# Expert layer of a decoder: the expert's columns as the stationary operand, and each tile's expert weights loaded into a ring of four

## The reference

```python
logits = x @ router_w + router_b
route = jax.nn.softmax(logits, axis=1)
max_prob = jnp.max(route, axis=1, keepdims=True)
max_ind = jnp.argmax(route, axis=1)
for e in range(num_experts):                    # 8
    h = x @ w1[e]                               # 128 -> 1024
    a, g = jnp.split(h, 2, axis=1)              # 512 each: "gate" a, "up" g
    y = jax.nn.silu(a) * g @ w2[e]              # 512 -> 128
    out = jnp.where((max_ind == e)[:, None], y, out)
out = out * max_prob                            # and the layer adds its input x
```

## Time and profile before

| what | value |
|---|---|
| median of 3 runs | 1973.05 us |
| profiled execution / its span | 1976.97 / 1975.2 us |
| PE, DVE, ACT, POOL busy, whole span | 1752.9, 1389.3, 1320.4, 854.7 us |
| expert phase: first row load issued / last output scatter | 1685.32 / 1966.79 us into the span |
| DMA over the whole span | 74.60 MB, mean 38 GB/s |

### The profile page before, as it was taken

The page is one execution under the profiler, slowest core; times in us unless marked ns, Lnnn a source line. Parts: engine busy times, 40 slices in busy tenths (PEclk is TensorE's granted clock), DMA queues, the critical chain, the costliest instruction groups (busy, mean ns, idle before and its releaser), DMA issues. The chain is left out here.

```text
span 1975.2 us, 52932 instructions
## 1 busy us (share of the span) xinstructions
PE 1752.9 (89%) x13247; PEld 1494.5 (76%) x13248; DVE 1389.3 (70%) x4484; ACT 1320.4 (67%) x3660; POOL 854.7 (43%) x2194
## 2 busy tenths in 40 slices
PE   5777679999997999979999999699999994788887
PEld 3444468888886999967888888588888883677776
DVE  5777658878876888866887887588888885233332
ACT  4444368888884777757888887588888883333343
POOL 1222044554541222224555453467877776133232
PEclk9999779999998999988999999899999997899999
DMA  8980000000000000000000000001111110111110
GB/s 233 391 345 0 1 14 12 12 13 12 12 11 2 0 0 0 0 1 1 0 0 0 0 0 1 21 24 28 34 32 31 32 33 31 30 35 33 33 33 21
DMA packets 76443, 74.60 MB, mean 38 GB/s; under 512 B 33077, under 2 KB 61896, under 8 KB 76368
## 3 DMA queue, kind: packets, MB, share of 16 engines
q1 hardware_dynamic: 71760, 64.85, 10.2%
q0 software_dynamic: 4320, 8.53, 1.2%
q10 hardware_dynamic: 288, 0.34, 0.1%
HBM read 30.02 MB, written 44.12 MB: 38 GB/s over the span
## 5 line engine op out<-in xcount | busy, mean ns | idle before, releaser
L1039 PE MATMUL xa_ps_o<-xa_vb,xa_pt 128*128 128x96 f32 x2048 | 246.6, 274 | 0.0
L1039 PEld LDWEIGHTS xa_ps_o<-xa_vb,xa_pt 128*128 128x128 f32 x2048 | 239.4, 192 | 0.1
L884 ACT ACTIVATE xa_pt<-xa_ps_pt 128x512 f32<-128x512 f32 x256 | 139.1, 595 | 96.5 <-PE xa_ps_pt L958 96.5
L1206 PE MATMUL ffn_ps_h<-ffn_xdt,w1t 128*128 128x128 f32 x1536 | 184.4, 276 | 0.4 <-ACT ffn_xdt L1172 0.4
L1287 DVE TENSOR_TENSOR exp_hg<-exp_silu,exp_ps_u 128x256 f32<-128x256 f32 x142 | 59.8, 421 | 174.0 <-ACT exp_silu L1272 174.0
L696 DVE TENSOR_REDUCE xa_mx<-xa_ps_s 128x8 f32<-128x512 f32 x256 | 164.9, 686 | 22.5 <-PE xa_ps_s L974 19.0
L1206 PEld LDWEIGHTS ffn_ps_h<-ffn_xdt,w1t 128*128 128x128 f32 x1536 | 178.9, 194 | 0.7 <-ACT ffn_xdt L1172 0.7
L848 POOL TENSOR_TENSOR xa_km<-xa_kt,const_sb 128x256 f32<-128x256 f32 x256 | 152.6, 617 | 36.5 <-ACT xa_kt L897 28.7
L702 DVE TENSOR_TENSOR xa_pr<-xa_ps_s,xa_mx 128x512 f32<-128x512 f32 x256 | 163.6, 680 | 0.2
L974 PE MATMUL xa_ps_s<-xa_km,xa_qm 64*128 64x256 f32 x1024 | 149.0, 410 | 4.0 <-POOL xa_km L848 4.0
L878 ACT ACTIVATE xa_pr<-xa_pr 128x512 f32<-128x512 f32 x256 | 147.2, 622 | 3.7 <-DVE xa_pr L702 0.8
(11 more groups left out here) (273 smaller groups left out, 4708.4 us busy)
## 6 DMA issues: line engine op xcount, KB each, us to landing
x_sorted<-no_row SPq DMA_DIRECT2D x1, 34320.0 KB, 91.2
xa_cn<-in_ctx_dram SPq DMA_DIRECT2D x128, 64.0 KB, 1.8
exp_xg<-x_sorted SPq DMA_DIRECT2D x71, 66.0 KB, 1.8
w1e<-in_L_ffn_w_dram SPq DMA_DIRECT2D x1, 4096.0 KB, 14.4
xa_mi<-in_mask_BxSxS_ik_dram SPq DMA_DIRECT2D x128, 32.0 KB, 2.2
out_dram<-exp_y,exp_token POOLq DMA_INDIRECT x71, 2.3
x_sorted<-x_sb,place POOLq DMA_INDIRECT x64, 2.4
x_sb<-in_x_dram SPq DMA_DIRECT2D x1, 512.0 KB, 5.2
```

Source lines behind the costliest of these rows:

```text
L884: nc.scalar.activation(pt[:, 512 * hf:512 * hf + 512], ps_pt[hf][:, :], ACT.Copy).then_inc(s["pt_sb"], 1)
L1039: last = nc.tensor.matmul(ps_o[:, 2 * VW * g:2 * VW * g + av_w], pt[:, P * g:P * g + P], vb[(r + 1) % RING][:, 2 * VW * g:2 * VW * g + av_ ...
L1206: last = nc.tensor.matmul(ps_h[c][:, 0:P], k.w1t[:, j, c, :], xdt[:, :, j:j + S], start=j == 0, stop=j == 2)
```

## The change

In `experts` the roles of the operands in UP are swapped. A 128-column piece of the expert's w1 is now stationary and the transposed tile `xt` moves, so the result comes out with the inner channel on the partitions, as Y needs it for its stationary operand. The transposes of `hg` and the copy `ht` are gone. Gate and up each get a PSUM tile of their own (512 wide, four pieces of 128), silu and the product are one instruction each over 512 columns, and `xt`, `silu`, `hg`, `ps_g`, `ps_u` and `ps_y` are doubled. On DVE `xn` now stands ahead of `hg`, on ACT `xt` ahead of silu.

The experts' weights no longer stay in SBUF. For each tile SP reads the owner's number and loads that expert's w1 (128 rows of 4 KB) and w2 (128 x 4 rows of 512 bytes) into one of four slots, for tile t+3 in turn t, once Y of tile t-1 has read the slot. PE waits for both loads before UP. The two loads of all experts in the first phase are gone, and with them the two register reads on PE.

```diff
+WRING = 4
 def load_weights(nc, k, a, sp):
-    sp.dma_start(k.w1e[:, :].rearrange("p (e f) -> p e f", e=E), a["L1_ffn_w1"].rearrange("e d f -> d e f")
-                 ).then_inc(k.expert_weights, 16)
-    sp.dma_start(k.w2e[:, :].rearrange("p (e c n) -> p e c n", e=E, c=FC),
-                 a["L1_ffn_w2"].rearrange("e (c p) n -> p e c n", p=P)).then_inc(k.expert_weights, 16)
...
             def _(sp):
                 def body(t, r):
...
                         sp.dma_start(xg[(r + 4) % XRING][:, :], k.x_sorted[bass.ds(first, P), :]).then_inc(s[f"x_in{r % 2}"], 16)
+                    if live(t + 3):
+                        e = sp.value_load(k.owner[0:1, col(t + 3)], min_val=0, max_val=E - 1)
+                        q = (r + 3) % WRING
+                        wait(sp, s["y_done"], t)
+                        sp.dma_start(w1b[q][:, :], w1[bass.ds(e, 1), :, :].rearrange("one d f -> d (one f)")
+                                     ).then_inc(s[f"w_in{q}"], 16)
+                        sp.dma_start(w2b[q][:, :, :], w2[bass.ds(e, 1), :, :].rearrange("one (c p) n -> p (one c) n", p=P)
+                                     ).then_inc(s[f"w_in{q}"], 16)
...
             def _(pe):
...
+                    if live(t + 1):
+                        q = (r + 1) % 2
+                        w = w1b[(r + 1) % WRING]
+                        pe.wait_ge(s["t_sb"], t + 2)
+                        pe.wait_ge(s[f"w_in{(r + 1) % WRING}"], 8 * (t + 1 - (r + 1) % WRING) + 32)
+                        wait(pe, s["hg"], t)
+                        for c in range(FC):
+                            last = nc.tensor.matmul(ps_g[q][:, c * P:(c + 1) * P], w[:, c * P:(c + 1) * P], xt[q][:, :],
+                                                    start=True, stop=True)
+                        last.then_inc(s["gate_done"], 1)
+                        for c in range(FC):
+                            last = nc.tensor.matmul(ps_u[q][:, c * P:(c + 1) * P], w[:, F + c * P:F + (c + 1) * P], xt[q][:, :],
+                                                    start=True, stop=True)
+                        last.then_inc(s["up_done"], 1)
                     if live(t):
-                        pe.wait_ge(s["hg"], 2 * t + 2)
-                        wait(pe, s["ht_sb"], t)
+                        q = r % 2
+                        pe.wait_ge(s["hg"], t + 1)
+                        wait(pe, s["y_sb"], t - 1)
                         for c in range(FC):
-                            last = nc.tensor.transpose(ps_ht[:, c * P:(c + 1) * P], hg[:, c * P:(c + 1) * P],
-                                                       k.const[:, C_ID:C_ID + P])
-                        last.then_inc(s["ht_done"], 1)
...
+                            last = nc.tensor.matmul(ps_y[q][:, 0:D], hg[q][:, c * P:(c + 1) * P], w2b[r % WRING][:, c, :],
                                                     start=c == 0, stop=c == FC - 1)
                         last.then_inc(s["y_done"], 1)
```

More of the change, by code:

```diff
@@ L948, in _ @@
                 if route:
-                    pe.wait_ge(k.expert_weights, 64)
+                    pe.wait_ge(k.expert_weights, 32)
                 kv = P if cross else 0
@@ L1213, in _, with experts @@
                 pipeline(pe, nt, 5, body, unroll=4)
-def experts(nc, k, out):
+def experts(nc, k, out, w1, w2):
     nt = k.nt
@@ L1230, in ps @@
             return ctx.enter_context(nc.psum_tensor("exp_ps_" + name, [P, w], F32))
-        half = F // 2
         xg = [sb(f"xg{i}", [P, R]) for i in range(XRING)]
+        w1b = [sb(f"w1b{i}", [P, 2 * F]) for i in range(WRING)]
+        w2b = [sb(f"w2b{i}", [P, FC, D]) for i in range(WRING)]
         xn = sb("xn", [P, D])
[L1234 to L1237, removed]
+        xt = [sb(f"xt{i}", [P, P]) for i in range(2)]
+        sa = [sb(f"silu{i}", [P, F]) for i in range(2)]
+        hg = [sb(f"hg{i}", [P, F]) for i in range(2)]
         y = [sb(f"y{i}", [P, D]) for i in range(2)]
@@ L1240, in experts @@
         token = [sb(f"token{i}", [P, 1], I32) for i in range(2)]
+        ps_g = [ps(f"g{i}") for i in range(2)]
         ps_u = [ps(f"u{i}") for i in range(2)]
-        ps_t, ps_ht, ps_y = (ps(n) for n in ("t", "ht", "y"))
-        names = ["x_in0", "x_in1", "xn", "t_done", "t_sb", "up_done", "silu", "hg", "ht_done", "ht_sb", "y_done", "y_sb",
-                 "carried", "stored0", "stored1"]
+        ps_y = [ps(f"y{i}") for i in range(2)]
+        ps_t = ps("t")
+        names = ["x_in0", "x_in1", "xn", "t_done", "t_sb", "gate_done", "up_done", "silu", "hg", "y_done", "y_sb",
+                 "carried", "stored0", "stored1"] + [f"w_in{i}" for i in range(WRING)]
         s = {n: k.sem("exp_" + n) for n in names}
@@ L1263, in body @@
                 def body(t, r):
[L1264 to L1273, removed]
                     if live(t + 2):
                         act.wait_ge(s["t_done"], t + 3)
-                        wait(act, s["up_done"], 2 * t + 4)
-                        nc.scalar.activation(xt[:, :], ps_t[:, 0:P], ACT.Copy).then_inc(s["t_sb"], 1)
+                        wait(act, s["up_done"], t + 1)
+                        nc.scalar.activation(xt[r % 2][:, :], ps_t[:, 0:P], ACT.Copy).then_inc(s["t_sb"], 1)
+                    if live(t + 1):
+                        q = (r + 1) % 2
+                        act.wait_ge(s["gate_done"], t + 2)
+                        wait(act, s["hg"], t)
+                        nc.scalar.activation(sa[q][:, :], ps_g[q][:, :], ACT.Silu).then_inc(s["silu"], 1)
                 pipeline_ring(act, ne, 4, body, XRING)
@@ L1282, in body @@
                 def body(t, r):
[L1283 to L1288, removed]
                     if live(t + 3):
@@ L1295, in body @@
                                                 ALU.subtract, ALU.mult).then_inc(s["xn"], 1)
+                    if live(t + 1):
+                        q = (r + 1) % 2
+                        dve.wait_ge(s["silu"], t + 2)
+                        dve.wait_ge(s["up_done"], t + 2)
+                        wait(dve, s["y_done"], t)
+                        nc.vector.tensor_tensor(hg[q][:, :], sa[q][:, :], ps_u[q][:, :], ALU.mult).then_inc(s["hg"], 1)
                     if live(t):
@@ L1300, in body @@
                         dve.wait_ge(s["y_done"], t + 1)
-                        nc.vector.scalar_tensor_tensor(y[q][:, :], ps_y[:, 0:D], row[:, GATE:GATE + 1], row[:, 0:D],
+                        nc.vector.scalar_tensor_tensor(y[q][:, :], ps_y[q][:, 0:D], row[:, GATE:GATE + 1], row[:, 0:D],
                                                        ALU.mult, ALU.add)
@@ L1327, in _ @@
             def _(pe):
-                def expert(n):
-                    return pe.value_load(k.owner[0:1, col(n)], min_val=0, max_val=E - 1)
                 def body(t, r):
[L1333 to L1336, removed]
                     if live(t + 2):
@@ L1374, in _ @@
             def _(sp):
-                sp.wait_ge(k.expert_weights, 64)
+                sp.wait_ge(k.expert_weights, 32)
                 sp.wait_ge(k.zeroed, 16)
@@ L1401, in decoder @@
         k.w2t = sb("w2t", [P, FC, P], BF16)
-        k.w1e = sb("w1e", [P, E * 2 * F])
-        k.w2e = sb("w2e", [P, E * FC * D])
         k.router_w = sb("router_w", [P, E])
@@ L1439, in decoder @@
         if 6 in phases:
-            experts(nc, k, out)
+            experts(nc, k, out, a["L1_ffn_w1"], a["L1_ffn_w2"])
         else:
```

## The result

| | before | after |
|---|---|---|
| median us (lowest to highest) | 1971.42 (1969.74 to 1973.36), 4 runs | 1927.72 (1926.38 to 1931.23), 4 runs |
| profiled execution / its span | 1976.97 / 1975.2 | 1931.23 / 1929.4 |
| a turn in the loop | 3.85 | 3.19 |

The ratio is 0.9773 [0.9757, 0.9789]: faster, inside the range, and 16 us above the 1912 forecast. A turn is read from SP's w1 issues over whole loops of eight turns: 1726.86 to 1880.13 is 153.27 us for 48 turns.

What follows compares the result with a forecast made beforehand. A ring of waits through PE, ACT and DVE bound the turn at 3.85 us; with SP pacing at 2.95, the last UP comes 62.1 us earlier (2.5 start loss included), the tail saves 1.6, in all 63.7: forecast 1912, range 1897 to 1948.

Steps and rivals of the forecast that it cites:

- The old ring of waits: One turn's chain of transposes, UP, silu, `hg` and `xn`, 3.85 us; PE's wait for `xn`, 0.41 a turn, was to go.
- PE at 24 passes of 0.110 and a transpose, 2.80: PE's need per turn after the change: 16 UP and 8 Y passes, 2.64 us, plus a transpose of 0.11 to 0.20.
- SP's own instructions pace, 2.95: SP's two register reads and three issues a turn set the pace at 2.95 us (2.84 to 3.2); chance 0.56.
- the term 0.08: Estimated SP time in us for the address of the third issue in a turn, beside 0.34 for the issue.
- The ring is wide enough: The four weight slots: freed slot to the end of Y takes 10.3 us over four turns, 2.6 a turn.
- The landing of the weights: Each tile's weight loads: 1.57 us, from a row load's landing, plus 2.16 us of moving the bytes.
- theory B: Experiments' theory: SP's wait for a transpose, the row issue behind it and the weights' load, back to PE two turns later.
- The DMA engines need 2.62 a tile: DMA work per tile in us: w1 1.28, w2 0.88, rows and output 0.46; under SP's 2.95 but near it.
- The tail and the start: Start: UP of tile 0 at 1691.5 instead of 1688.93, 2.5 us lost; tail, last UP to `y`: 1.6 less.
- PE paces: Rival: SP's issues stay cheap, so PE sets a turn of 2.75 to 2.84 us, about 1902; chance 0.10.
- DMA paces: Rival: issues wait for loads ahead and pieces move at 298 GB/s, turn 3.1 to 3.8 us; 1944 at 3.4; chance 0.24.
- SP is not held till weights have landed: Denies the slower rival: SP held until each tile's weights land, turn 4.6 us, 2029, held `router_w` for it; chance 0.07.

Runs made afterwards that it cites:

- no_reload: Changed kernel with weights loaded for the first four tiles only, later tiles using the slots as they are: 1901.10 us, 0.9625 of the kernel before.
- deep_ring8_y4: Changed kernel with weights issued first, rows six tiles ahead from ACT, a ring of eight, and four y and token buffers instead of two: 1900.72 us.
- half_w1: Changed kernel loading only the gate half of w1, which the up matmuls read again: 1918.75 us, 0.9721 of the kernel before.
- extra_read: Changed kernel with the owner's number read a second time on SP in each turn: 1957.24 us, 0.9908 of the kernel before.
- deep_rows_sp: Changed kernel with SP issuing weights first, then rows six tiles ahead with four semaphores: 1921.20 us, 0.9726 of the kernel before.
- deep_w2_2k: deep_rows_act with w2 loaded as one 2 KB piece per partition instead of four of 512 bytes: 2036.52 us, 1.0319 of the kernel before.
- deep_rows_act: Changed kernel with rows six tiles ahead issued by ACT and the weights alone by SP: 1911.00 us, 0.9678 of the kernel before.

## Why the prediction was right or wrong, point by point

- *The old ring of waits goes*: right. No wait of PE for `xn`; silu and `hg` are never last.
- *PE at 24 passes of 0.110 and a transpose, 2.80*: right. 2.79 in every turn without a stall, and throughout no_reload and deep_ring8_y4. That PE's idle time would be ended by the weights is right too, but it is 14.2 us of 190 by PE's busy time (20.6 by the starts of its matmuls), 0.24 to 0.35 a turn where 0.15 was expected.
- *SP's own instructions pace, 2.95*: the mechanism was right, the term 0.08 too small, which is 0.08 x 70 = 5.6 us of the miss. half_w1 and extra_read show 3.03 and SP as the pace. An issue was well read (0.33, 0.33 and 0.38 us, estimated from the earlier trace rows). Too small was the third issue with its address: 0.34 + 0.08 = 0.42 was put, and from the end of w1's issue to the end of w2's it is 1810.22 - 1809.65 = 0.57; with the two loads at 1.21 that gives 2.99. The loop's end, once in eight turns (in half_w1's loop w1 issues are 2.88 to 3.05 apart, across its end 3.6), was in the sum: the 1.21 is a mean over turns of before, where SP's time from one wait to the next is 1.13 to 1.17 in most turns and about 1.6 across the loop's end.
- *The ring is wide enough*: right as far as the slots go, since SP never waits for one in after. *The landing of the weights, 1.57 us behind the issue plus the move, 3.73 in all*: this is the step that failed. It took the landing time of a row load from an idle queue; under load both weights land 4.8 us behind w1's issue in the median, and a row load in 3.0, not 1.8. The prediction names the loop that this feeds (an SP that waits for a transpose issues rows and weights late, and PE, two tiles on, waits for them) but gives it no price. In after's trace a transpose is followed by the row issue after 0.44 us, when SP waits for it, by w1's issue after another 1.16 to 1.2, by the landing after 4.8 and by `gate` after 0.09; the next transpose starts 2.68 behind `gate`. That is 9.2 us over three turns, 3.06 a turn, level with SP's 3.03; with 3.73 for the landing it would be 2.7. The sum took the largest of its limits, but these two share waits: SP comes late in some turns (the loop's end), landings vary from 4.2 to 6.0, and what one loses the other does not give back. Read on SP, the 3.19 is its own 3.03, 0.11 of waiting for the transpose (theory B; deep_rows_sp is without it and gains 6.5 us), and 0.04 because the read of `first_row` lasts longer than in half_w1 (337 ns against 289 in the mean from 1700 to 1890, 270 before). Why it does was not tested. Its minimum, median and maximum, in ns, before and after:

```profile
L1256 SPq TENSOR_LOAD <-first_row x49: 263/269/280, 1702.5 to 1888.3; - x49
L1249 SPq TENSOR_LOAD <-first_row x59: 263/271/500, 1702.2 to 1887.1; - x59
```

- *The DMA engines need 2.62 a tile*: not too low. At the 387 GB/s of deep_ring8_y4's first stretch 920 KB take 2.4 us, and at a share of 0.93 in after more would still fit. The row read for pieces of 512 bytes, the load of x, has packets of 2048 bytes in the trace, but the term stands: after's own 512-byte packets take 27 ns, on 16 engines 303 GB/s.
- *The tail and the start*: 1.5 us gained where 1.6 was put, and 3.1 lost where 2.5 was.
- *Rivals*: PE paces only once SP and the landings are taken out of the way. (What was held against this rival has an exception: one static issue of the first phase, at 21.63, took 0.27.) DMA paces is ruled out by half_w1 and deep_ring8_y4. SP is not held till weights have landed: in after's loop it issues rows 1.45 us behind a w2 that lands in 4.1, and no issue there lasts over 0.39. The held `router_w` was no guide to that, and not the only held issue of the first phase: others took 8.76 us (at 9.00) and 2.96 (at 27.55). The estimate of 8.0 us a turn from the Trainium skill, "DMA: Bandwidth & Descriptors" ("Anatomy of one DMA"), does not hold here: loads overlap, and a turn is 3.19. That section is about DMAs issued by GpSimd, and these are issued by SP.

The remaining steps from the changed kernel down to PE's floor, in medians: rows deeper, 6.5 us; rows off SP, 10.2; ring of eight, 5.0; four `y` buffers, 5.3; in all 27.0, to 1900.72. By the ratios, each to the kernel before beside it, they are about 9, 9, 6 and 6. The last two are each near what their runs can tell apart; that ring of eight and `y` buffers together bring about 10 is clear of both intervals.

## What to carry to other kernels

Where one engine issues all loads of a turn, add up its own instructions first, every address and the loop's end included, and take landing times from loads under the traffic that the change will make. Where two or three limits lie within a tenth of each other and share waits, the turn can be longer than the largest (here 3.03, 3.06 and 2.79 made 3.19); deeper buffers at each place that waits for a landing bring it down to that one. A DMA share near 1.0 is no proof that the DMA engines pace: halve the bytes or deepen the buffers and see.

## What the runs showed of the hardware that was not expected

- A stationary operand whose 128 float32 columns lie four apart loads in 326 ns instead of 194, and a pass takes 0.233 us instead of 0.111 (deep_w2_2k).
- At a DMA share of 0.98 to 1.08 nearly the same mix of loads moved between 309 and 387 GB/s (deep_rows_act, deep_ring8_y4).
- One register read on SP, with the check of its bounds, costs 0.55 to 0.59 us (extra_read), more than a DMA issue (0.33 to 0.38). The read alone takes 0.27 before and up to 0.50 in after.
